# A three-layer perceiver block on one core: w_down turned behind the last projection from kept blocks, and other orders at two places of the program

## The reference

```python
x = x + cross_attention(layernorm(x), ctx)   # 16 heads of 64, K and V from the 257 keys, Wo and bo
x = x + self_attention(layernorm(x))         # in each batch of 32 tokens, 16 heads of 64, relative bias, Wo
x = x + ffn(layernorm(x))                    # all three weights and both inputs fake-quantized to 8 bits

def ffn(x, clip_x, clip_down, w_gate, w_up, w_down):
    xq = act_fake_quant(x, clip_x)           # one scale for the whole tensor, from max |x|
    gate = xq @ weight_fake_quant(w_gate).T  # 512 -> 1408, one scale for each output row
    up = xq @ weight_fake_quant(w_up).T
    h = act_fake_quant(silu(gate) * up, clip_down)   # one scale for the whole tensor again
    return h @ weight_fake_quant(w_down).T   # 1408 -> 512
```

## Time and profile before

| what | value |
|---|---|
| median of three runs | 1605.65 us (1605.06 to 1606.41) |
| the profiled execution's own time | 1601.76 us |
| its span in the trace | 1600.0 us |
| busy: PE, DVE, ACT, POOL | 1548.1, 1072.9, 732.2, 372.2 us (97, 67, 46, 23%) |
| chain that ended last | PE 74%, issue 11%, DVE 9%, ACT 4%, DMA 1% |
| granted clock, mean | 0.988 of 2.4 GHz |

### The profile page before, as it was taken

The page is one execution under the profiler, slowest core; times in us unless marked ns, Lnnn a source line. Parts: engine busy times, 40 slices in busy tenths (PEclk is TensorE's granted clock), DMA queues, the critical chain, the costliest instruction groups (busy, mean ns, idle before and its releaser), DMA issues.

```text
span 1600.0 us, 36060 instructions
## 1 busy us (share of the span) xinstructions
PE 1548.1 (97%) x13778; PEld 1286.6 (80%) x13778; DVE 1072.9 (67%) x2314; ACT 732.2 (46%) x1589; POOL 372.2 (23%) x225
## 2 busy tenths in 40 slices
PE   7999879999999999999999999999999999996989
PEld 6888668888989899888989899878878788784444
DVE  7766677776667766776667766556565565555788
ACT  5544645555545554555545554433222222223755
POOL 1000343343444344343444344400000000000000
PEclk9999989999999999999999999999999999997999
DMA  6898862431333223331334223240311312242022
GB/s 245 319 366 327 330 243 109 137 135 59 138 132 140 74 106 136 136 134 59 138 134 138 76 104 122 97 181 22 120 54 40 114 41 66 100 157 97 1 105 106
DMA packets 80047, 213.63 MB, mean 134 GB/s; under 512 B 5776, under 2 KB 31824, under 8 KB 77136
## 3 DMA queue, kind: packets, MB, share of 16 engines
q1 hardware_dynamic: 79952, 212.27, 36.9%
HBM read 141.86 MB, written 70.39 MB: 133 GB/s over the span
## 4 chain that ended last, share of the span: by engine, by line
PE 74%; issue 11%; DVE 9%; ACT 4%; DMA 1%; POOL 0%; DVEq 0%; SPq 0%; ACTq 0%; POOLq 0%
PE psum_o L674 13%; PE psum_s L651 7%; PE psum_q L651 6%; PE psum_o L1451 6%; PE psum_q L1491 6%; PE psum_q L1451 6%; PE psum_t L1520 6%; PE psum_o L539 5%; PE psum_o L689 5%; DVE qk L1070 3%; PE psum_t L662 3%; PE psum_t L620 2%; PE psum_s L1478 1%; PE psum_t L571 1%; PE psum_q L571 1%
## 5 line engine op out<-in xcount | busy, mean ns | idle before, releaser
L674 PE MATMUL psum_o<-pT,c_nat 128*128 128x512 f32 x1152 | 307.3, 403 | 1.0 <-DVE pT L935 0.7
L674 PEld LDWEIGHTS psum_o<-pT,c_nat 128*128 128x128 f32 x1152 | 202.7, 188 | 36.1 <-DVE pT L935 1.0
L1273 POOL TENSOR_TENSOR c_nat<-c_raw,constants 128x768 fp32r<-128x768 f32 x64 | 94.9, 1483 | 574.4 <-PE psum_o L674 460.3
L1136 DVE TENSOR_SCALAR oT<-psum_o,c_last 128x512 f32<-128x512 f32 x192 | 143.9, 749 | 66.7 <-PE psum_o L674 66.6
L651 PE MATMUL psum_s<-cT,qk 128*128 128x256 f32 (+1 forms) x1152 | 168.8, 289 | 11.2 <-DVE cT L935 9.3
L651 PEld LDWEIGHTS psum_s<-cT,qk 128*128 128x128 f32 x1152 | 152.1, 191 | 20.3 <-DVE cT L935 14.1
L864 ACT ACTIVATE probs<-psum_s,nmax 128x257 f32<-128x257 f32 x128 | 61.1, 477 | 205.2 <-DVE nmax L1151 205.2
L651 PE MATMUL psum_q<-cT,qk 128*128 128x256 f32 (+1 forms) x1152 | 152.2, 283 | 0.7 <-DVE qk L1070 0.7
L651 PEld LDWEIGHTS psum_q<-cT,qk 128*128 128x128 f32 x1152 | 143.0, 190 | 3.5 <-issue 2.6
L935 DVE TENSOR_TENSOR pT<-psum_t,pT 128x512 fp32r<-128x512 f32 x128 | 87.8, 687 | 70.9 <-ACT pT L755 70.9
L1258 POOL TENSOR_TENSOR c_raw<-c_raw,last_row 128x768 f32<-128x768 f32 x64 | 120.2, 1879 | 22.2 <-DMA last_row<-in_ctx_dram 22.2
(11 more groups left out here) (273 smaller groups left out, 3120.3 us busy)
## 6 DMA issues: line engine op xcount, KB each, us to landing
qk_by_tile<-staged SPq DMA_DIRECT2D x32, 1536.0 KB, 10.2
raw<-qk_by_tile SPq DMA_DIRECT2D x16, 3072.0 KB, 12.3
c_raw<-in_ctx_dram SPq DMA_DIRECT2D x64, 384.0 KB, 3.2
last_row<-in_ctx_dram SPq DMA_DIRECT2D x64, 192.0 KB, 3.9
out_dram<-x_out SPq DMA_DIRECT2D x32, 256.0 KB, 2.0
x_res<-in_x_dram SPq DMA_DIRECT2D x16, 256.0 KB, 2.7
x_in<-out_dram SPq DMA_DIRECT2D x4, 1024.0 KB, 8.3
x_res<-out_dram SPq DMA_DIRECT2D x16, 256.0 KB, 2.9
```

Of the source, the lines that this page charges most:

```text
L674: i = pe.matmul(ps[:], c_nat[(b - 1) % 2][:, part, k, m * P:(m + 1) * P], pT[:, moving, k, :], start=(k, part, moving) == (0, 0, 0), stop= ...
L1136: nc.vector.tensor_scalar(oT[:, m, :, (b - 1) % 4, :], ps[:].rearrange("p (s q) -> p s q", q=SQ), c_last[:, (b - 1) % 2, m:m + 1], None, A ...
L1273: G.tensor_tensor(flat(c_nat[i][:, 0, :, :]), flat(c_raw[i][:]), zero.to_broadcast([P, 2 * DC]), ALU.add).then_inc(s_chi, 1)
```

## The change

At the border of the first tile DVE rounds the first low part of the next queries ahead of the first attended output, brings the last context chunk and the norms ahead of the two last low parts, and ACT its share of that chunk ahead of the two last high parts. POOL's first run in the second tile waits until all four low parts are there, and takes the subtraction before the split. SP loads the context of the second tile's first step before `wo_raw`, `wv`, `bo_all` and `x_res`, not behind them.

The four rounded blocks of w_down stay in SBUF (three `wd_whole`, the fourth in `wd_front` and `wd_back`). Their 44 transposes leave the loop of the last self group, and with them go eight copies on DVE, four stores and the load of `wdT`. They stand now behind the last projection on PE, in six groups, and ACT copies each group from PSUM into its place in `wdT`.

In the last self group PE makes the attended values of tile 2 before the last product of V, and those of tile 3 inside the projection of tile 2; the projection of tile 3 has a bank and an operand of its own (`t1`, `aT2_last`). DVE and ACT follow that order, and the residuals of the last two tiles come in one early load. The 3 MB load of normed tiles is split in three of 1 MB; the second and third are issued after the last projection, since their place holds `aT2_last` and the kept blocks until then. In the loop of gate and up the first of 11 units is made in two halves of 256 tokens, the first when q0 is copied and the second when q1 is.

The core of the diff:

```diff
+def first_units():
+
+    return x_units() + [(("ROW",), "t0")] + [(("DT", g), ("s0", "s1", "o0", "o1", "s0", "t1")[g]) for g in range(6)]
...
+        wd_whole = [nc.alloc_sbuf_tensor_at(f"wd_whole{n}", [P, HID], BF16, offset=at)
+                    for n, at in enumerate((IN2, IN2 + 2 * HID, BETWEEN))]
...
+        wd_front = nc.alloc_sbuf_tensor_at("wd_front", [P, WD_CUT], BF16, offset=IN2 + 4 * HID)
+        wd_back = nc.alloc_sbuf_tensor_at("wd_back", [P, P], BF16, offset=BETWEEN + 2 * HID)
...
                 act_last_scalars(act, t, b, section)
+                if b == 3 and not begun:
+                    ctxT(b, 2)
...
                 if b == 3 and more:
                     act_qk_high(act, t + 1, 2)
                     act_qk_high(act, t + 1, 3)
-                if after:
+                if after and (b < 3 or begun):
                     ctxT(b, 2)
...
-                if qk_next and begun:
+                if qk_next:
                     dve_qk_low(dve, t + 1, 0, section)
                 dve_attended(dve, t, b, 0, section)
                 inverse(b, 3)
-                if qk_next and begun:
+                if qk_next and not begun:
+                    ctxT(b, 0)
+                    ctxT(b, 1)
+                    dve_qk_low(dve, t + 1, 1, section)
+                    norm(b, 2)
+                    norm(b, 3)
+                    ctxT(b, 2)
+                    dve_attended(dve, t, b, 1, section)
+                    dve_qk_low(dve, t + 1, 2, section)
+                    dve_qk_low(dve, t + 1, 3, section)
+                    dve_attended(dve, t, b, 2, section)
+                    continue
+                if qk_next:
                     dve_qk_low(dve, t + 1, 1, section)
                 if after:
                     ctxT(b, 0)
                     ctxT(b, 1)
-                if qk_next and not begun:
-                    dve_qk_low(dve, t + 1, 0, section)
-                    dve_qk_low(dve, t + 1, 1, section)
                 norm(b, 2)
...
+                if section == "second" and b == 0:
+                    pool.wait_ge(s_qlo, 4 * t + 4)
+                    pool_less_last(pool, t, b + 1)
+                    pool_split(pool, t, b, section)
+                    continue
...
-            sp.dma_start(wo_raw[:], Wo.rearrange("(k p) n -> p k n", p=P)).then_inc(s_wo, 16)
             full(sp, U1(("CT", 0, 2), 0, "first"))
             sp.wait_ge(s_nat, 2)
             load_ctx(sp, 0, 3)
             load_qk(sp, 0, 1)
+            sp.wait_ge(s_nat, 3)
+            load_ctx(sp, 0, 4)
+            sp.dma_start(wo_raw[:], Wo.rearrange("(k p) n -> p k n", p=P)).then_inc(s_wo, 16)
             sp.dma_start(wv[:], Wv.rearrange("(k p) n -> p k n", p=P)).then_inc(s_wvo, 16)
             sp.dma_start(bo_all[:], bo.rearrange("(a n) -> a n", a=1).to_broadcast([P, D])).then_inc(s_wvo, 16)
             sp.dma_start(x_res[:], rows(x_rows, 0)).then_inc(s_xres, 16)
-            for b in range(2, 4):
-                sp.wait_ge(s_nat, b + 1)
-                load_ctx(sp, 0, b + 2)
+            sp.wait_ge(s_nat, 4)
+            load_ctx(sp, 0, 5)
...
+        def pe_turn_down(pe):
+
+            pe.wait_ge(s_wround, FC + KD + 1)
+            for g in range(6):
+                ps, done = empty(pe, U3(("DT", g), 0, "first"))
+                for a in down_blocks(g):
+                    m = pe.transpose(bf16_blocks(ps, 2 * D)[:, a % 8, :], wd_block(a // FC, a % FC), ident16[:])
+                m.then_inc(done, 1)
...
+                if last:
+                    pe_self_attended(pe, s, 2)
+                    pe_self_v(pe, s, 3, 1)
+                    pe_self_out(pe, s, 2, range(KI // 2))
+                    pe_self_attended(pe, s, 3)
+                    pe_self_out(pe, s, 2, range(KI // 2, KI))
+                    pe_self_out(pe, s, 3)
...
+            n = c - FC
+            act.wait_ge(s_dclamp, n + 1)
+            if n < KD - 1:
+                nc.scalar.activation(wd_whole[n][:], wd_stage[:], ACT.Copy, bias=-ROUND).then_inc(s_wround, 1)
             else:
-                act.wait_ge(s_dclamp, c - FC + 1)
-                nc.scalar.activation(wd_nat[:], wd_stage[:], ACT.Copy, bias=-ROUND).then_inc(s_wround, 1)
+                nc.scalar.activation(wd_front[:], wd_stage[:, 0:WD_CUT], ACT.Copy, bias=-ROUND).then_inc(s_wround, 1)
+                nc.scalar.activation(wd_back[:], wd_stage[:, WD_CUT:], ACT.Copy, bias=-ROUND).then_inc(s_wround, 1)
...
+                else:
+                    dve_self_probs(dve, s, 3, ch)
+                    dve_self_out(dve, s, 1, ch2)
+                    dve_self_attended(dve, s, 2)
                     dve_out_rsqrt(dve, slice(0, 2), ch2)
...
                     dve_out_norm(dve, s, slice(0, 2), ch2)
+                    dve_self_attended(dve, s, 3)
+                    dve_self_out(dve, s, 2, ch2)
                     dve_short_rsqrt(dve, 2, ch2)
                     dve_out_norm(dve, s, slice(2, 3), ch2)
...
+                    dve_self_out(dve, s, 3, ch2)
                     dve_short_rsqrt(dve, 3, ch2)
...
                     if not more and i == 0:
-                        sp.wait_ge(s_wgu, 16 * (FC + KD))
-                        sp.dma_start(wdT[:].rearrange("p c k n -> p c (k n)"), wd_dram.rearrange("c p n -> p c n")).then_inc(s_wguback, 16)
+                        sp.dma_start(x_res_last[:], x1_dram[(TILES - 2) * P:, :].rearrange("(t p) d -> p t d", p=P)).then_inc(s_xres_last, 16)
+                        sp.wait_ge(s_wgu, 16 * FC)
                         sp.dma_start(wguT[:].rearrange("p c w k n -> p c (w k n)"), wgu_dram.rearrange("c p n -> p c n")).then_inc(s_wguback, 16)
                         sp.wait_ge(s_x3st, 16 * (GROUPS - 1))
-                        sp.dma_start(xn3_all[:, 0:GROUP * (GROUPS - 1), :].rearrange("p (s t) d -> p s (t d)", t=GROUP),
-                                     xn3_dram.rearrange("s p n -> p s n")).then_inc(s_x3back, 16)
+                        sp.dma_start(xn3_all[:, 0:GROUP, :].rearrange("p t d -> p (t d)"), xn3_dram[0]).then_inc(s_x3back, 16)
+                    if not more and i == GROUP - 1:
+                        sp.dma_start(xn3_all[:, GROUP:2 * GROUP, :].rearrange("p t d -> p (t d)"), xn3_dram[1]).then_inc(s_x3later[0], 16)
+                        for g in range(6):
+                            full(sp, U3(("DT", g), 0, "first"))
+                        sp.dma_start(xn3_all[:, 2 * GROUP:3 * GROUP, :].rearrange("p t d -> p (t d)"), xn3_dram[2]).then_inc(s_x3later[1], 16)
...
+            def products(i, w, ps, part):
+                later = xqT[:, :, part.start:]
+                for k in range(KD):
+                    m = pe.matmul(ps[:, part], wguT[:, i, w, k, :], later[:, k, bass.ds(n * 512, part.stop - part.start)],
+                                  start=k == 0, stop=k == KD - 1)
+                return m
+
+            first = 1 if section == "loop" else 0
+            places = [empty(pe, U3(("GU"[w], i), n, section)) for i in range(first) for w in range(2)]
+            for half, b in enumerate(("q0", "q1")):
                 pe.wait_ge(drained[b], U3.before(b, n, section, 1))
-            for i in range(FC):
+                for i in range(first):
+                    for w in range(2):
+                        ps, done = places[2 * i + w]
+                        m = products(i, w, ps, slice(256 * half, 256 * half + 256))
+                        if half:
+                            m.then_inc(done, 1)
+            for i in range(first, FC):
                 for w in range(2):
                     ps, done = empty(pe, U3(("GU"[w], i), n, section))
-                    for k in range(KD):
...
-            pe.wait_ge(s_wguback, 32)
+            pe_turn_down(pe)
+            pe.wait_ge(s_wguback, 16)
...
+            for g in range(5):
+                act_down_turned(act, g)
...
             act_copy(act, U3(("ROW",), 0, "first"), row[:])
+            act_down_turned(act, 5)
             act.wait_ge(s_gu, 1)
             act.wait_ge(s_out, 16 + 32 * TILES)
+            for s in s_x3later:
+                act.wait_ge(s, 16)
```

More of the change, by code:

```diff
@@ L1566, in pe_self_all @@
                 pe_self_v(pe, s, 1, 1)
-                for i in range(GROUP):
+                last = s == GROUPS - 1
+                for i in range(2 if last else GROUP):
                     pe_self_attended(pe, s, i)
@@ L1801, in dve_turned @@
                 dve.wait_ge(s_wgu, 16 * c)
[L1802 to L1807 removed]
+            ps, free = full(dve, own(("GUT", c)))
+            nc.vector.tensor_scalar(w_turned[:], bf16_blocks(ps, 2 * D), 1.0, None, ALU.mult).then_inc(free, 1)
         def dve_weight(dve, name):
@@ L1980, in pe_ffn @@
             pe_gate_up(pe, NCH - 1, "last")
+            for g in range(6):
+                taken(pe, U3(("DT", g), 0, "first"))
             for n in range(NCH):
@@ L2043, in act_gate_up, with act_down_turned @@
                         act_x_take(act, i // 2 - 3, n, section, n + 1)
```

(5 more changed lines are left out.)

141 lines of the change are left out of this document (74 added, 67 removed).

## The result

The changed kernel takes 1582.55 us (four executions, 1582.19 to 1583.30) against 1605.36 us; the ratio is 0.9864, 95% interval 0.9850 to 0.9879. On a second occasion it was 1583.43 against 1604.27 us, 0.9869 (0.9854 to 0.9884). Forecast were 1588.2 and a range down to 1584.0. The way is right, 17.4 us were promised and some 21 to 23 came. Its profiled execution took 1582.19 us, 19.6 under the one that the prediction read; the rest of the miss lies between a profiled execution and the median.

A forecast was written before the change was run, and what follows sets the result against it. TensorE, busy 97% of the span at mean clock 0.988, was taken as the bound. Terms -8.1 - 2.9 - 5.5 - 1.2 + 0.3 = -17.4 from 1601.76 gave 1584.4, plus 3.9 gave 1588.2 us; range 1584.0 to 1593.5.

The forecast's parts named there:

- The border: First tile's border: VectorE's new order brings TensorE's first product with the context to 238.8 instead of 246.89, 8.1 us less.
- the loop: Last self group: four iterations lose w_down's transposes, 0.73 us each, 2.9 us less in all.
- the tail: End of the last self group: new order takes 17.0 us instead of 22.50, 5.5 less; 3.5 if one stall stays.
- rival A: First border gives only part: GpSimd catches the norms, +2.8, or maximum-to-product time stays 4.88, +1.8; 1591.0 us, chance 0.15.
- D: Feed-forward start: ScalarE's five copies or the transposes come late and tokens wait, +1 to +3; 1590 to 1591, chance 0.06.
- Rival C: Gate and up loop's head: third load of normed tiles late, up to 12.3 us lost, 1600.5; chance 0.05 with other losses.
- The 3.09 us: Second tile's start: undisturbed time from first maximum to TensorE's first product with the context, taken instead of 4.88.
- the median of the runs shown is 3.9 above it, which I keep: Whole kernel: before's median lay 3.9 us above its profiled 1601.76; the same 3.9 was added to 1584.4.
- the start of the feed-forward layer: From last projection to gate and up: 1.2 us less from the halved first unit, 0.3 more for extra products.
- The halves: First unit of gate and up: end comes 1.2 us sooner; extra products in two later rounds cost 0.3.
- rival B: Feed-forward start: the clock doesn't fall, 3.0 us on the path saved, 1585.2 us; chance 0.12.
- The loads at the border: First border: earlier load of the next context removes a 1.45 us stall, counted as no further gain; some 0.4 lost otherwise.

The follow-up runs named there:

- the changed kernel again: The changed kernel timed a second time with no edit: 1583.43 us, ratio 0.9869; border stretch 29.04 us in its profile.
- the fills: Unused transposes in TensorE's waits: changed kernel with old border and tail orders, 1597.78 to 1593.10 us; with old border orders and new loads, 1590.96 to 1588.37.
- the other profile of before: The kernel before, run again with no edit: profiled execution 1601.11 us, median 1603.46 us, ratio 1.0003.
- The fill: The changed kernel with 76 more unused transposes on TensorE in the wait for the tokens: 1581.23 us, ratio 0.9853.

## Why the prediction missed

**The border, the loop, the tail: right, in place and size, against the execution that was read.** -8.06, -2.99 and -5.44 for -8.1, -2.9 and -5.5. VectorE's rebuilt order was met to 0.2 us, the cover of the copies in the tail held, and neither rival A nor D came: GpSimd ended 1.7 us before the norms. ScalarE's copies ended at 1448.08, 0.09 before the tokens' first operation there. Rival C had nothing: no wait for a load at the loop's head.

Two things in this were luck. The 3.09 us from the first maximum to TensorE's product with the context ends in the earlier trace rows at 256.10, which is a reciprocal of VectorE's and no product; TensorE's product of that step came at 262.87, behind those with wv. What the product does wait for, VectorE's second copy into `pT`, ended just there (before, then the changed kernel, where the product starts at 238.95), so 3.25 was measured:

```profile
255.50 0.68 DVE L935 TENSOR_TENSOR pT<-psum_t,pT 128x512 fp32r<-128x512 f32 x1
```

```profile
238.17 0.68 DVE L957 TENSOR_TENSOR pT<-psum_t,pT 128x512 fp32r<-128x512 f32 x1
```

And -8.06 is one pair of executions: with the 29.04 of the changed kernel again it is -6.45, and in the medians the border is worth 6.5 (alone in before) to 8.2 (undone).

**The step that failed is "the median of the runs shown is 3.9 above it, which I keep".** The 3.9 was taken for a constant of the measurement. It is none: in the changed kernel the median lies 0.4 above the profiled execution at first and 0.5 below it again. So 3.5 of the 5.65 us missed were in that step. Some of the 3.9 was the draw of three executions: on the later occasions before's medians were 1603.5 to 1604.3, 1.7 to 2.5 above 1601.76. Some of it goes with the places that the change takes away: behind a wait TensorE worked for some microseconds at half clock, more in one execution and less in another; the context came 1.45 to 3.85 us late and the last w_down load 1.5 later or not. With the same orders the border took 35.49 to 39.58 in five profiles of old orders and old loads, the tail 22.29 to 24.17 in six, and the profile read for the prediction had the least border, almost the least tail and the least wait for w_down. That these places cost more than their waits, by the clock, is shown by the fills: 4.7 us in the median with the waits left in place, 2.6 at the border alone. The loads' part is shown in profiles but not told apart in the medians. How much of the 3.9 the three places make is not shown: the other profile of before had 3.1 more in the border and the wait for w_down, and took 0.65 less in all, by less half clock ahead of the border and behind the last result.

**The other 2.2 are the start of the feed-forward layer and the last stage, -0.9 forecast and 0 for -2.19 and -0.86.** Part of it is again the execution read, which had the longest of both among four profiles with the old start (95.66 to 97.31 and 42.96 to 43.99). Ten with the new start, unit in halves and nothing filled there, have 93.80 to 95.15 and 42.91 to 43.13; the means are 2.0 and 0.6 apart, but against before's other profile the two rows would be -0.54 and +0.17. The halves gave 1.4 up to the second unit (1473.44 and 1455.43, less the 16.64 by which the projection ended sooner) for 1.2, the added products nothing to be seen for 0.3. The rest is rival B by half: the clock fell again but for a shorter time. The fill puts a price of 1.9 on what is left, for the rival's 3.0. Why it is shorter, and why the last stage mostly has less half clock too, was not settled: no kernel took the transposes out of that wait alone.

**The loads at the border** were given nothing in the forecast; with the new orders the medians give them 0.8 to 1.7, inside the intervals, and each profile with the old loads has the wait.

## What to carry to other kernels

A wait of the busiest engine can cost more than its length where the clock falls behind it: look at the granted clock of the stretch behind it and count the work done there at the lower level. One profile is one draw; before a distance between it and the median is carried over to a changed kernel, take a second profile, ask which waits could make the distance, and whether the change removes them. Two engines that slow each other down are best set one after the other: without GpSimd's wait the border lost 4.8 of the 8.2 us that its new orders bring.

## What the runs showed of the hardware

Useless work can pay: 144 transposes whose result nobody reads, in two waits of TensorE, take the changed kernel from 1582.55 and 1583.43 to 1580.54 us. And a load of a given size and place was not of one duration: the 704 KB of the last w_down block landed 4.0 us behind their issue in one execution of before and 5.6 in another. The clock was not the same either: 0.71 or 1.00 over 200 to 205 us, behind the same wait of 2.5 us, in two executions of one kernel.
